# Two gate projections ahead of two x projections in each pair of a Mamba mixer kernel

## The chip, the cores and the metric

The kernel runs on one core of a Trainium2 chip. The metric is the device time of one execution in microseconds (us), lower is better. Five engines work side by side, each through its own list of instructions in order: PE is TensorE (matmuls), DVE is VectorE, ACT is ScalarE, POOL is GpSimd, and SP is SyncE, which issues the DMAs here. They wait for each other by counting semaphores.

## The reference

A residual stream x of 4 sequences of 256 tokens with 512 channels goes through a feed-forward layer, a Mamba2 mixer, and the same feed-forward layer again. Nearly all of the time is the mixer:

```python
proj = hidden_states @ in_proj_w.T
gate, xBC, dt = jnp.split(proj, [INTER, INTER + CONV_DIM], axis=-1)
...
xBC = jax.nn.silu(jnp.swapaxes(conv, 1, 2))
x, Bm, Cm = jnp.split(xBC, [INTER, INTER + NG * SS], axis=-1)
y = _ssd(x.reshape(Bsz, S, NH, HD), Bm.reshape(Bsz, S, NG, SS), Cm.reshape(Bsz, S, NG, SS), D, dt, dt_bias)
y = y.reshape(Bsz, S, INTER)
yg = y * jax.nn.silu(gate)
yg_g = yg.reshape(Bsz, S, NG, GROUP)
rstd = jax.lax.rsqrt(jnp.mean(jnp.square(yg_g), axis=-1, keepdims=True) + EPS)
out = (yg_g * rstd).reshape(Bsz, S, INTER) * norm_w
return out @ out_proj_w.T
```

INTER is 8192, in 8 groups of 1024 channels. `conv` is a causal convolution of 4 taps over the tokens, and `_ssd` the scan in chunks of 128 tokens, which inside a chunk is a product of a decay matrix, B and C, and x.

## The kernel before

The mixer goes through the 8 groups g. A group is 16 steps in 8 pairs j (`pair(g, j)`), and a tail (`tail`). A step is one tile of 128 channels of x and of the gate for half of the tokens (512 columns); the two steps of a pair, a = 2j and b = 2j + 1, are the two halves of one tile. Every engine has a `pair` and a `tail` of its own, which say in which order that engine does its work; nothing else orders it.

A projection is 12 matmuls of 128x512 (4 pieces of the contraction by three passes that split float32 into a high and a low part, `three_pass`, L166 to L168). There are two kinds in a pair:

- An x unit (`ip.project`, L923) writes bank 0 or 1. ACT starts the convolution (`evacuate`, L961), DVE adds three taps (`taps`, L976), ACT takes the tanh (L1337), DVE makes the silu (`silu_conv`, L1519) and turns the tile (L1529). It is sent out to HBM and comes back as `xd`, and POOL scales it (`scale_x`, L1253). The x units of a pair are those that the next pair mixes: steps 2j + 2 and 2j + 3. In the last pair of a group they are the next group's B and C units.
- A gate (`project_gate`, L1711) writes one of the two banks of `TG_BANK`. ACT takes the tanh (L1365) and DVE makes the silu (`silu_gate`, L1554). It waits for the weights (`wlo`), for the silu of the gate two steps before (`sg`), and, for the first two steps of a group, for `ms`, since the tail uses the same banks for sums (`turn_sums`, L1768), which DVE's `mean_square` reads (L1568) and whose last instruction (L1572) raises `ms`:

```python
pe.wait_ge(s["wlo"], 1 + WPG * g + w + 1)
if st < 2:
    pe.wait_ge(s["ms"], 1 + g)
if not (first(g) and st < 2):
    pe.wait_ge(s["sg"], 1 + STEPS * g + st - 1)
```

After these four PE does two output projections (`project_out`, 12 matmuls each; in group 0 there are none in pairs 0 to 3), for which POOL must have gated y (`gate_y`, L1232) and split the tile (`split_tile`, L1237), and then `mix_tokens` for a and b (L1737, L1741), which needs DVE's `make_mix` (L1540), ACT's decays (L1348, L1358) and `xd`. DVE then forms y (`skip_y`, L1548).

DVE's list for a pair is: `skip_y` of the two steps before, `make_mix` of a, `taps` of both x units, `make_mix` of b, then for each of the two a `silu_conv`, a `silu_gate` and a turn, then `split_wo` (L1558), and, in pairs 0 to 3, the sums `add_quads` and `add_group` (L995, L1002) of two tiles. In pair 0 both `make_mix` come ahead of the taps. In the tail it is: `skip_y` twice, constants, then

```python
taps(g + 1, 4)
taps(g + 1, 5)
mean_square(g)
```

and the silus of units 4 and 5. POOL's list for a pair is: two masks (L1224), `gate_y` twice, `split_tile` twice, `scale_x` twice, a mask (L1217), a weight remainder (L920), a mask, a weight remainder, and the squares' sums (L1245).

Of the kernel before, what the change touches and what calls it, by code (L numbers as in the profile page):

```python
# [163 lines left out]
def three_pass(nc, out, w_hi, w_lo, x_hi, x_lo, first, last):  # L164

    nc.tensor.matmul(out, w_hi, x_hi, start=first, stop=False)  # L166
    nc.tensor.matmul(out, w_hi, x_lo, start=False, stop=False)  # L167
    return nc.tensor.matmul(out, w_lo, x_hi, start=False, stop=last)  # L168
# [656 lines left out]
def first(g):  # L825

    return isinstance(g, int) and g == 0
# [205 lines left out]
def mixer_phase(nc, m, ip, norm_w, w_out, ncs_dram, x_dram, next_ln, sums, early):  # L1033

    with ExitStack() as ctx:
# [67 lines left out]
        def units_of(g, j):  # L1103

            if j < PAIRS - 1:
                return [(g, 2 * j + 6), (g, 2 * j + 7)]
            return [(g + 1, 0), (g + 1, 1)] if g + 1 < NG else []
# [12 lines left out]
        def has_tile(g, p):  # L1120
            return p >= XT or not first(g)
# [570 lines left out]
        def _(pe):  # L1692
# [18 lines left out]
            def project_gate(g, st):  # L1711
                w, hf = 3 + 2 * (st // 2), st % 2
# [5 lines that stand above are left out]
                at = slice(hf * HALF, (hf + 1) * HALF)  # L1718
                for k in range(KT):
                    last = three_pass(nc, TG_BANK[st % 2][:, :], w_hi[:, w % 3, k, :], w_lo[:, w % 3, k, :],  # L1720
                                      m.h_hi[:, k, at], m.h_lo[:, k, at], k == 0, k == KT - 1)
                last.then_inc(s["gate"], 1)

            def mix_tokens(g, st):

                i = st % 2
                x_scaled(pe, g, st)
                pe.wait_ge(s["mix"], 1 + STEPS * g + st + 1)
                if st == 0:
                    pe.wait_ge(s["cbt"], 1 + 2 * g + 1)  # L1730
                else:
                    pe.wait_ge(s["ysb"], 1 + STEPS * g + st - 1)
                for b in range(HB):
                    c0 = b * SEQ
                    for hd in range(2):
                        rows = slice(hd * HD, (hd + 1) * HD)
                        nc.tensor.matmul(Y_BANK[i][rows, c0:c0 + SEQ], xd[:, i, rows, 2 * b],  # L1737
                                         mix[:, i, hd, b, 0:SEQ], start=True, stop=False)
                    for hd in range(2):
                        rows = slice(hd * HD, (hd + 1) * HD)  # L1740
                        last = nc.tensor.matmul(Y_BANK[i][rows, c0 + CH:c0 + SEQ], xd[:, i, rows, 2 * b + 1],  # L1741
                                                mix[:, i, hd, b, SEQ:PAIR], start=False, stop=True)
                last.then_inc(s["y"], 1)

            def project_out(g, p):

                q = tile_of_step(p)[0]
                i, bank = p % 2, O_BANK[p % 2]
                pe.wait_ge(s["ylo"], 1 + STEPS * g + p + 1)
                pe.wait_ge(s["wolo"], 1 + XT * g + (QUAD if q == 0 else 0))  # L1750
                if p > XT + 1:
                    pe.wait_ge(s["gcopy"], 1 + TT * g + p - XT - 1)
                elif p >= 2:
                    pe.wait_ge(s["gsum"], 1 + TT * g + p - 1)
                elif g == NG:
                    pe.wait_ge(s["gcopy"], 1 + TT * g - 1 + p)
                else:
                    pe.wait_ge(s["cbt"], 1 + 2 * g + 2)
                for r in range(QUAD):
                    last = three_pass(nc, bank[:, :], yt_hi[:, i, r, :], yt_lo[:, i, r, :],  # L1760
                                      wo_hi[:, QUAD * q + r, :], wo_lo[:, QUAD * q + r, :], r == 0, r == QUAD - 1)
                last.then_inc(s["out"], 1)
# [13 lines left out]

            def pair(g, j):
                steps = (2 * j, 2 * j + 1)
                for u in units_of(g, j):
                    ip.project(pe, *u)  # L1780
                for st in steps:
                    project_gate(g, st)
                for p in steps:
                    if has_tile(g, p) and not (g == NG - 1 and p == STEPS - 1):
                        project_out(g, p)
                for st in steps:
                    mix_tokens(g, st)

            def tail(g, more):
# [9 lines left out]
                else:  # L1799
# [9 lines left out]
                    project_out(NG, 7)  # L1809

            groups_in_turn(pair, tail)


# [56 lines left out]
```

## Time and profile before

| | |
|---|---|
| median of 3 runs | 1524.92 us (1524.83 to 1527.4) |
| the profiled execution | 1522.31 us, its span 1520.5 us |
| PE busy | 1477.9 us |
| DVE busy | 1290.9 us |
| POOL busy | 1155.5 us |
| ACT busy | 1015.2 us |
| mean granted clock of PE | 0.991 of full |

Busy time is the time in which an engine has an instruction under way. Times in the rows are microseconds from the start of the span. A row of the timeline has the start, the time taken, the engine, the line in the kernel, the operation, what it writes and reads, and how many are merged; the square bracket at its end gives how long the engine had been idle and who released it.

### The profile page before, as it was taken

What the parts mean: (1) busy time and instruction counts of PE and PEld (TensorE: products, weight loads), DVE (VectorE), ACT (ScalarE), POOL (GpSimd) and SP (SyncE); (2) the same over time, 40 slices, a digit from 0 to 9 for tenths busy, and PEclk for the clock granted to TensorE, in tenths of its full rate; (3) what the DMA queues carried; (4) which work ended last, traced back from release to release, by engine and by line L of the source; (5) the groups of instructions that cost most, each with busy time, mean ns of one, the idle gap of its engine ahead of it and who ended that gap; (6) DMA issues with size and microseconds to landing.
All of it is one profiled execution on the core that took longest, in us unless ns stands there. A gap on an engine that the chain in (4) does not pass through costs nothing. (4 is left out here: it accounts for less than half of the span.)

```text
span 1520.5 us, 24373 instructions
## 1 busy us (share of the span) xinstructions
PE 1477.9 (97%) x7720; PEld 1212.3 (80%) x7720; DVE 1290.9 (85%) x1664; ACT 1015.2 (67%) x2154; POOL 1155.5 (76%) x917
## 2 busy tenths in 40 slices
PE   6979899999999999999999999999999999999988
PEld 4767788888888888888888888888888888888766
DVE  6689987998789987998789977998799987998675
ACT  4366777667766777667766677667766777667540
POOL 3017997699958997699959997699859997699830
PEclk9989999999999999999999999999999999999999
DMA  3026542444435442444434442544434442544201
GB/s 126 1 84 193 181 155 89 160 158 149 139 104 160 148 152 84 160 159 154 132 111 156 150 153 77 172 152 151 143 100 162 150 151 74 180 149 141 99 15 56
DMA packets 165680, 198.79 MB, mean 131 GB/s; under 512 B 21040, under 2 KB 86576, under 8 KB 165296
## 3 DMA queue, kind: packets, MB, share of 16 engines
q1 hardware_dynamic: 165552, 197.22, 39.5%
q8 instruction: 63, 1.03, 0.3%
q14 instruction: 65, 0.53, 0.1%
HBM read 160.98 MB, written 36.18 MB: 130 GB/s over the span
## 5 line engine op out<-in xcount | busy, mean ns | idle before, releaser
L166 PE MATMUL bank<-h_hi,mx_w_hi 128*128 128x512 f32 x1152 | 459.4, 399 | 4.4 <-DVE mx_acc L1519 2.8
L167 PE MATMUL bank<-h_lo,mx_w_hi 128*128 128x512 f32 x1152 | 450.3, 391 | 0.0
L168 PE MATMUL bank<-h_hi,mx_w_lo 128*128 128x512 f32 x1152 | 449.7, 390 | 0.0
L976 DVE SCALAR_TENSOR_TENSOR mx_acc<-bank,mx_cw,mx_acc 128x510 f32<-128x510 f32 (+2 forms) x480 | 353.9, 745 | 43.1 <-ACT mx_acc L961 29.9
L1540 DVE TENSOR_TENSOR mx_mix<-mx_mix,mx_cbt 128x1536 f32<-128x1536 f32 x128 | 266.0, 2083 | 37.0 <-ACT mx_mix L1358 37.0
L1348 ACT ACTIVATE mx_mix<-mx_csb,ncs 128x256 f32<-128x256 f32 x512 | 217.9, 498 | 111.1 <-PE bank L1741 109.1
L1232 POOL TENSOR_TENSOR mx_y<-mx_y,mx_sg 128x512 f32<-128x512 f32 x128 | 248.5, 1962 | 19.0 <-DVE mx_y L1548 19.0
L166 PEld LDWEIGHTS bank<-h_hi,mx_w_hi 128*128 128x128 f32 x1152 | 217.4, 189 | 56.0 <-POOL mx_w_lo L920 4.1
L168 PEld LDWEIGHTS bank<-h_hi,mx_w_lo 128*128 128x128 f32 x1152 | 217.1, 188 | 46.4
L167 PEld LDWEIGHTS bank<-h_lo,mx_w_hi 128*128 128x128 f32 x1152 | 217.6, 189 | 42.5
L920 POOL TENSOR_TENSOR mx_w_lo<-mx_w_raw,mx_w_hi 128x512 fp32r<-128x512 f32 x144 | 191.7, 1332 | 74.3 <-ACT mx_w_hi L915 73.8
L166 PE MATMUL bank<-mx_wo_hi,mx_yt_hi 128*128 128x512 f32 x512 | 201.0, 393 | 2.9 <-POOL mx_yt_lo L1237 2.9
L168 PE MATMUL bank<-mx_wo_hi,mx_yt_lo 128*128 128x512 f32 x512 | 200.2, 391 | 0.0
L167 PE MATMUL bank<-mx_wo_lo,mx_yt_hi 128*128 128x512 f32 x512 | 199.2, 389 | 0.0
L1217 POOL TENSOR_SCALAR_AFFINE_SELECT mx_csb<-mx_csb 128x512 f32<-128x512 f32 x128 | 119.6, 934 | 100.1 <-DMA mx_csb<-cs_rows 99.6
L1253 POOL TENSOR_TENSOR mx_xd<-mx_xd,mx_gdt 128x512 f32<-128x512 f32 x128 | 165.8, 1315 | 38.6 <-DMA mx_xd<-x_squares 38.6
L1237 POOL TENSOR_TENSOR mx_yt_lo<-mx_y,mx_yt_hi 128x512 fp32r<-128x512 f32 x128 | 167.2, 1325 | 30.4 <-ACT mx_yt_hi L1371 30.2
L1358 ACT ACTIVATE mx_mix<-mx_mix,ncs 128x128 f32<-128x128 f32 x512 | 162.7, 390 | 39.0 <-POOL mx_mix L1224 38.9
L1245 POOL TENSOR_TENSOR mx_ssum<-mx_ssum,mx_sq 128x512 f32<-128x512 f32 x112 | 175.0, 1582 | 0.1
L1737 PE MATMUL bank<-mx_mix,mx_xd 128*64 128x256 f32 x1024 | 163.4, 397 | 3.9 <-issue 3.1
L961 ACT ACTIVATE mx_acc<-bank,mx_cb,mx_cw 128x512 f32<-128x512 f32 x160 | 123.5, 773 | 53.4 <-PE bank L168 35.6
L1548 DVE SCALAR_TENSOR_TENSOR mx_y<-mx_acc,mx_dh,bank 128x512 f32<-128x512 f32 x128 | 92.4, 742 | 72.7 <-PE bank L1741 72.7
(172 smaller groups left out, 2236.8 us busy)
## 6 DMA issues: line engine op xcount, KB each, us to landing
mx_csb<-cs_rows SPq DMA_DIRECT2D x128, 512.0 KB, 4.1
mx_w_raw<-in_w_in SPq DMA_DIRECT2D x144, 256.0 KB, 3.7
x_squares<-mx_th SPq DMA_DIRECT2D x128, 256.0 KB, 2.0
mx_xd<-x_squares SPq DMA_DIRECT2D x512, 64.0 KB, 2.0
mx_wo_raw<-in_w_out SPq DMA_DIRECT2D x64, 256.0 KB, 4.2
res<-in_x SPq DMA_DIRECT2D x8, 256.0 KB, 4.4
out<-res SPq DMA_DIRECT2D x8, 256.0 KB, 2.0
f_base_raw<-in_base_wt SPq DMA_DIRECT2D x1, 1024.0 KB, 7.2
```

Of the source, the lines that this page charges most:

```text
L166: nc.tensor.matmul(out, w_hi, x_hi, start=first, stop=False)
L167: nc.tensor.matmul(out, w_hi, x_lo, start=False, stop=False)
L168: return nc.tensor.matmul(out, w_lo, x_hi, start=False, stop=last)
L920: self.nc.gpsimd.tensor_tensor(self.w_lo[:, w % 3, :, :], self.w_raw[:, w % 3, :, :], self.w_hi[:, w % 3, :, :].bitcast(F32), ALU.subtract ...
L976: self.nc.vector.scalar_tensor_tensor(dst, src[:, :, 0:SEQ - k], self.cw[:, c, TAPS - 1 - k:TAPS - k], dst, ALU.mult, ALU.add).then_inc(s[ ...
L1232: nc.gpsimd.tensor_tensor(y[:, st, :], y[:, st, :], sg[:, st % 2, :], ALU.mult).then_inc(s["yg"], 1)
L1237: nc.gpsimd.tensor_tensor(yt_lo[:, p % 2, :, :], y_tile(q, hf, t), yt_hi[:, p % 2, :, :].bitcast(F32), ALU.subtract).then_inc(s["ylo"], 1)
L1245: nc.gpsimd.tensor_tensor(ssum[:, i, :], ssum[:, i, :], sq[:, i, :], ALU.add).then_inc(s["ssum"], 1)
L1253: nc.gpsimd.tensor_tensor(a, a, gdt[:, hf, 2 * j:2 * j + 2, :].unsqueeze(2).to_broadcast([P, 2, HD, 2 * HB]), ALU.mult).then_inc(s["xd"], 1)
L1348: nc.scalar.activation(mix[:, i, hd, b, 0:SEQ], csb[:, i, hd, b * SEQ:(b + 1) * SEQ], ACT.Exp, bias=m.ncs[:, tile, head:head + 1], scale=-1.0)
L1540: nc.vector.tensor_tensor(a, a, both, ALU.mult).then_inc(s["mix"], 1)
L1737: nc.tensor.matmul(Y_BANK[i][rows, c0:c0 + SEQ], xd[:, i, rows, 2 * b], mix[:, i, hd, b, 0:SEQ], start=True, stop=False)
```

## The change

In PE's list for a pair, the two gate projections are written ahead of the two x units instead of behind them. No other engine's list changes, and no wait is added or removed.

```diff
             def pair(g, j):
                 steps = (2 * j, 2 * j + 1)
+                for st in steps:
+                    project_gate(g, st)
                 for u in units_of(g, j):
                     ip.project(pe, *u)
-                for st in steps:
-                    project_gate(g, st)
                 for p in steps:
                     if has_tile(g, p) and not (g == NG - 1 and p == STEPS - 1):
                         project_out(g, p)
```

PE's list where a tail ends and pair 0 of the next group begins (L1706 and L1707 are the last work of the tail; `mx_tap`, `mx_wlo`, `mx_sg` and `mx_ms` are the semaphores `tap`, `wlo`, `sg` and `ms`), before:

```order
L1706 MATMUL bank<-mx_acc 128x256 [waits mx_gcopy,mx_conv]
L1707 MATMUL bank<-mx_acc 128x128
L1706 MATMUL bank<-mx_acc 128x256
L1707 MATMUL bank<-mx_acc 128x128
L166 MATMUL bank<-h_hi,mx_w_hi 128x512 [waits mx_tap,mx_wlo]
L167 MATMUL bank<-h_lo,mx_w_hi 128x512
L168 MATMUL bank<-h_hi,mx_w_lo 128x512
```

And with the change:

```order
L1706 MATMUL bank<-mx_acc 128x256 [waits mx_gcopy,mx_conv]
L1707 MATMUL bank<-mx_acc 128x128
L1706 MATMUL bank<-mx_acc 128x256
L1707 MATMUL bank<-mx_acc 128x128
L166 MATMUL bank<-h_hi,mx_w_hi 128x512 [waits mx_sg,mx_ms,mx_wlo]
L167 MATMUL bank<-h_lo,mx_w_hi 128x512
L168 MATMUL bank<-h_hi,mx_w_lo 128x512
```

The first projection of the group was an x unit that waits for taps; now it is a gate that waits for `ms`. In the other pairs the last projection ahead of the output projections was a gate, before:

```order
L167 MATMUL bank<-h_lo,mx_w_hi 128x512
L168 MATMUL bank<-h_hi,mx_w_lo 128x512
L166 MATMUL bank<-h_hi,mx_w_hi 128x512 [waits mx_sg,mx_wlo]
L167 MATMUL bank<-h_lo,mx_w_hi 128x512
L168 MATMUL bank<-h_hi,mx_w_lo 128x512
```

And with the change it is the x unit of step b, which waits for the silu of the unit two before it (`mx_conv`):

```order
L167 MATMUL bank<-h_lo,mx_w_hi 128x512
L168 MATMUL bank<-h_hi,mx_w_lo 128x512
L166 MATMUL bank<-h_hi,mx_w_hi 128x512 [waits mx_conv,mx_wlo]
L167 MATMUL bank<-h_lo,mx_w_hi 128x512
L168 MATMUL bank<-h_hi,mx_w_lo 128x512
```

## Rows read from the trace of the kernel before

**Rows 1.** The page's busy time of each engine.

```profile
PE 1477.9 (97%) x7720; PEld 1212.3 (80%) x7720; DVE 1290.9 (85%) x1664; ACT 1015.2 (67%) x2154; POOL 1155.5 (76%) x917
```

**Rows 2.** Busy time by stretches; last three columns are clock, DMA share, GB/s.

```profile
173.40:1423.80 1250.40, 1250.36 (x6642) 1034.85 (x6640) 1098.74 (x1289) 878.77 (x1891) 1056.58 (x828) 1.00 0.43 140
```

**Rows 3.** Who waited for whom: total us, times, longest.

```profile
ACT mx_w_hi L915 <- PE bank L168: 88.6, 51, 2.2
```

**Rows 4.** Timeline of PE, pair 6 of group 3 and the next start.

```profile
724.08 0.50 PE L166 MATMUL bank<-h_hi,mx_w_hi 128*128 128x512 f32 x1
...
735.09 0.39 PE L166 MATMUL bank<-mx_wo_hi,mx_yt_hi 128*128 128x512 f32 x1
...
740.66 0.71 PE L1737 MATMUL bank<-mx_mix,mx_xd 128*64 128x256 f32 x4
...
743.52 0.50 PE L166 MATMUL bank<-h_hi,mx_w_hi 128*128 128x512 f32 x1
```

**Rows 5.** Timeline of ACT and DVE in the same pair.

```profile
729.85 0.78 ACT L961 ACTIVATE mx_acc<-bank,mx_cb,mx_cw 128x512 f32<-128x512 f32 x1 [0.35 <-PE bank L168]
...
730.66 2.31 DVE L976 SCALAR_TENSOR_TENSOR mx_acc<-bank,mx_cw,mx_acc 128x510 f32<-128x510 f32 x3 [0.41 <-ACT mx_acc L961]
732.89 2.26 DVE L1540 TENSOR_TENSOR mx_mix<-mx_mix,mx_cbt 128x1536 f32<-128x1536 f32 x1
...
735.67 0.67 DVE L1554 SCALAR_TENSOR_TENSOR mx_sg<-mx_sg,bank 128x512 f32<-128x512 f32 x1
...
739.36 1.12 DVE L1558 SCALAR_TENSOR_TENSOR mx_wo_lo<-mx_wo_raw,mx_nw,mx_wo_hi 128x512 fp32r<-128x512 f32 x1
```

**Rows 6.** Timeline of PE and DVE where group 4 begins.

```profile
777.45 0.48 PE L166 MATMUL bank<-h_hi,mx_w_hi 128*128 128x512 f32 x1
...
778.88 1.28 DVE L1568 TENSOR_REDUCE mx_rms<-bank 128x4 f32<-128x512 f32 x2
780.20 0.17 DVE L1572 TENSOR_SCALAR mx_rms<-mx_rms 128x8 f32<-128x8 f32 x1
```

**Rows 7.** The same place at the starts of groups 1 and 7.

```profile
267.16 0.48 PE L166 MATMUL bank<-h_hi,mx_w_hi 128*128 128x512 f32 x1
...
269.91 0.17 DVE L1572 TENSOR_SCALAR mx_rms<-mx_rms 128x8 f32<-128x8 f32 x1
...
1287.68 0.48 PE L166 MATMUL bank<-h_hi,mx_w_hi 128*128 128x512 f32 x1
...
1290.43 0.17 DVE L1572 TENSOR_SCALAR mx_rms<-mx_rms 128x8 f32<-128x8 f32 x1
```

**Rows 8.** Two idle times of PE in group 0, and a stretch's clock.

```profile
125.44 0.79 PE L166 MATMUL bank<-h_hi,mx_w_hi 128*128 128x512 f32 x1 [2.79 <-DVE mx_acc L1519]
...
129.84 0.40 PE L166 MATMUL bank<-h_hi,mx_w_hi 128*128 128x512 f32 x1
...
171.78 0.71 PE L1737 MATMUL bank<-mx_mix,mx_xd 128*64 128x256 f32 x4 [3.13 <-issue]
...
120.00:130.00 10.00, 7.21 (x43) 5.86 (x40) 9.41 (x14) 6.76 (x15) 7.39 (x8) 0.83 0.71 243
```

**Rows 9.** Timeline of group 0: DVE's first silu_gate, PE at pair 4.

```profile
123.19 0.68 DVE L1554 SCALAR_TENSOR_TENSOR mx_sg<-mx_sg,bank 128x512 f32<-128x512 f32 x1
...
173.41 0.80 PE L166 MATMUL bank<-h_hi,mx_w_hi 128*128 128x512 f32 x1
```

**Rows 10.** Timeline of DVE and POOL, pair 1 of group 4 into pair 2.

```profile
808.05 1.96 DVE L1540 TENSOR_TENSOR mx_mix<-mx_mix,mx_cbt 128x1536 f32<-128x1536 f32 x1
...
818.01 1.40 DVE L1548 SCALAR_TENSOR_TENSOR mx_y<-mx_acc,mx_dh,bank 128x512 f32<-128x512 f32 x2
...
818.84 4.08 POOL L1232 TENSOR_TENSOR mx_y<-mx_y,mx_sg 128x512 f32<-128x512 f32 x2 [1.62 <-DVE mx_y L1548]
822.86 2.58 POOL L1237 TENSOR_TENSOR mx_yt_lo<-mx_y,mx_yt_hi 128x512 fp32r<-128x512 f32 x2
```

**Rows 11.** Timeline of PE, the last pair of the last group.

```profile
1430.02 0.50 PE L166 MATMUL bank<-mx_wo_hi,mx_yt_hi 128*128 128x512 f32 x1 [0.48 <-POOL mx_yt_lo L1237]
```

## Prediction

> **What bounds the kernel now.** I read the page's busy times first: PE is busy 1477.9 us of 1520.5, far ahead of the others [rows 1]. Then I asked where its idle time lies. From pair 4 of group 0 to the last pair of group 7, 1250.4 us, PE is busy 1250.36 us at a granted clock of 1.00 [rows 2]. So for four fifths of the span PE's own work is the time: nothing can be gained there by order, and every wait that the change gives to PE is added in full. Next I read the timeline of one pair. It starts at 724.08, the four projections take 11.01 us (2.75 each), the output projections begin at 735.09, the mixing at 740.66, and the next pair starts at 743.52, 19.44 us after the first [rows 4]. Last I read, for each wait on PE, when it is satisfied today. Below, +n is the time since the start of a pair.
>
> **What the change does.** It removes and adds no instruction and no wait; PE, ACT, DVE, POOL and the DMA queue have the same work. Gates come 5.5 us earlier, x units 5.5 us later. ACT waits 88.6 us in all for PE ahead of a weight's rounding [rows 3], in good part because its list has that rounding behind the gates; those waits shorten, but with PE never idle in that stretch this is worth nothing, and ACT will wait ahead of its evacuations instead.
>
> *Term 1, the first gate of a group.* It waits for `ms`, raised by the last instruction of `mean_square`. At the start of group 4 the first projection runs at 777.45, while `ms` comes at 780.20 + 0.17 = 780.37, which is 2.92 us later [rows 6]. Today an x unit fills that time, whose taps are done. In group 1 the gap is 270.08 - 267.16 = 2.92 us and in group 7 1290.60 - 1287.68 = 2.92 us [rows 7]. The tail of each group is not reordered, and `mean_square` stands behind the taps of the last unit that the tail projects, so `ms` comes no earlier. PE's list is held at its head. The x units behind it are ready, but no row of this trace shows a matmul that passes one that waits. Seven group starts (1 to 7) by 2.92 give 20.4 us. Group 0 starts with `ms` free.
>
> The Trainium skill says of this ("TensorE: Matmul & The Clock Gate", the step-by-step part of Part 2) that matmuls stay in program order and only weight loads are pulled ahead. By that rule the term is the whole 20.4 us; if matmuls could pass each other it would be near nothing.
>
> *Term 2, the clock after such a gap.* PE was idle 2.79 us before 125.44, and the next projection took 129.84 - 125.44 = 4.40 us against 2.75, 1.65 us more; the stretch of 10 us around it has a mean granted clock of 0.83, so some 3.4 us at the lower level (1.2 GHz), 1.7 us of full-speed work lost [rows 8]. The gap of 3.13 us at 171.78 [rows 8] is followed by a first matmul of 0.80 us at 173.41 [rows 9], against 0.50 at 724.08 [rows 4]. So two of two gaps of this size in the mixer cost the clock. The new gap is 2.92 us. Bounds: nothing (each gap gets off) and 7 x 1.7 = 11.9; I take six of seven at 1.5, 9 us.
>
> The Trainium skill tells of such a loss paid at every pass of a loop ("TensorE: Matmul & The Clock Gate", HAM oscillation); its rule makes the loss hang on how long the gaps are. By it all seven would pay or hardly any; the two rows speak for paying.
>
> *Term 3, group 0, pairs 1 to 3.* Here there are no output projections to stand between the last x unit and the mixing. The mixing of b needs `make_mix` of b, which DVE has behind the taps of unit b. In pair 6 of group 3 the evacuation of unit b starts at 729.85, about 0.2 us after its projection, takes 0.78, the taps 2.3, `make_mix` 2.0 to 2.3 [rows 5]. With the unit's projection ending at +11.0, `make_mix` is done at about +16.3, the mixing of b (half of 743.52 - 740.66, 1.4 us [rows 4]) at +17.8. So these pairs take about 17.9 us. Pair 1 can begin when the first `silu_gate` is done, 123.19 + 0.68 = 123.9 [rows 9], instead of 125.44 [rows 8]; three pairs bring pair 4 to 177.6 instead of 173.41 [rows 9]: +4.2 us. PE is idle some 4 us in each of them, so the clock loss comes here too, about 1.2 each after what today's two gaps cost is gone: +8 us in all. Bounds -3 (the early start stays and the mixing is never late) and +12.
>
> *Term 4, output projections in pairs 2 to 4, groups 1 to 7.* DVE must now wait for the late x units and so does its later work later. From `make_mix` of b to the end of `skip_y` it takes 819.41 - 808.05 = 11.36 us where `add_quads` and `add_group` are in the list [rows 10]. `make_mix` of b starts at +14.3 (+11.0, 0.2, 0.78, 2.3 [rows 5]), so the first `skip_y` is done 24.9 us after the pair's start, +5.5 in the next. `gate_y` then takes 4.08 for two and the first split 1.3 [rows 10]: +10.9. PE wants it at +11.0 [rows 4]. The slack is 0.1 us. Today it is 3.1: the split is done at 822.86 + 1.3 = 824.2 [rows 10], +7.9 of a pair that starts at 777.45 + 2 x 19.44 = 816.3. POOL's list and its contention with DVE can shift it. There are 21 such pairs. Bounds: nothing, and 1 us each, 21; I take 0.15 each, 3 us, nearest the row.
>
> *Term 5, the last pair.* It has no x units, so its output projections want the split at about +5.6; today they start 0.48 us late, at 1430.02 [rows 11], which is +6.2. From `make_mix` of b to the end of `split_wo` DVE takes 740.48 - 732.89 = 7.6 us [rows 5]; +14.3 + 7.6 is +2.5 in the next pair, `skip_y` adds 0.7, `gate_y` and the first split 5.4: +8.6. That is 2.4 us later than today; I take 2.5. Bounds 0 and 5.
>
> *What stays covered.* In the other pairs, gate a needs `silu_gate` of the pair before: 3.45 us after the start of `make_mix` [rows 5], so at +17.8, ahead of 19.4. The mixing of b wants `make_mix` at +18.0 and gets it at about +16.5; the cover is the two output projections, 5.6 us, and without them it costs what term 3 says. The turned x of step a goes to its DMA soon after `silu_gate`, at about +19, and the mixing needs it at +16.6 of the next pair, 17 us on. The weights of a gate are split a pair ahead, those of x are now wanted later than before.
>
> The sum: 20.4 + 9 + 8 + 3 + 2.5 = 42.9 us. On the profiled execution, 1522.31 us, that is 1565.2. The median of the runs lies 2.6 us above the profiled one, so I forecast 1568 us.
>
> **Rivals.**
> - *The gap costs no clock.* 2.92 us may be too short in most groups, as it depends on what PE does around it. Then terms 2 and the clock's part of 3 fall away: 42.9 - 9 - 3.6 = 30.3, so 1555 us. For it: the gap of 2.92 is near the smaller of the two seen. Against: both of the two paid. Chance 0.22.
> - *POOL and DVE become the bound in pairs 1 to 4.* The slack of 0.1 us in term 4 is overrun by 1 us per pair, since POOL has two instructions of the same kind that take 1.3 us alone and 2 beside DVE [rows 10]. Then 28 pairs pay 1 us: 1568 - 3 + 28 = 1593 us. For it: POOL is busy 1056.58 us of 1250.4 [rows 2]. Against: that leaves 3 us per pair. Chance 0.12.
> - *Not slower: the gates fill group 0's holes and the group starts cost nothing.* If DVE reached `mean_square` 2.9 us earlier, relative to PE, than now, the first gate would find `ms` up. Then only group 0 changes: pair 1 starts 1.5 us earlier and its first projection keeps the clock, 1.65 us: 1522 us, 0.2% faster. It decides at 2.92 us of `ms` against the tail's end. Against it: three starts of groups, spread over the whole span, show the same 2.92 [rows 6, 7], and the tail's order is untouched. Chance 0.04, of which half would be within 0.2%.
>
> **How the numbers follow.** Forecast 0.62, rivals 0.22, 0.12, 0.04. The forecast's own spread is the bounds of term 2 (some 5 us down, 3 up), of term 3 (4 up) and of term 4 (10 up). The range 1549 to 1584 takes in the rival without clock loss and leaves out the other two, about 0.18. Measurements of this kernel tell 0.2%, 3 us, from no change. Slower 0.96, same 0.02, faster 0.02.
>
> **What would show it.** The waits of PE should have a new entry of about 2.9 us, seven times, the first matmul of a group released by DVE's L1572. The granted clock should show seven short falls between 260 and 1340 us. In group 0, PE should wait some 4 us ahead of L1737 in pairs 1 to 3, released by DVE's L1540. ACT's wait before L915 should shrink by some 50 us with PE no faster. Pair length in pairs 5 to 7 should stay at 19.44. I am wrong if `ms` is up when the tail ends, if pair lengths between group starts grow (POOL), or if the gaps leave the clock at 1.00.

## The result and the profile after

The changed kernel takes 1567.58 us (median of 4 runs, 1563.96 to 1569.85), the kernel before 1525.66 us on the same chip (4 runs, 1524.83 to 1527.40). The ratio is 1.0271, 95% interval [1.0248, 1.0294]: 2.7% slower. The forecast was 1568 us, range 1549 to 1584. The profiled execution of the changed kernel took 1568.67 us, with a span of 1566.9 us at a mean granted clock of 0.984; before, 1520.5 us at 0.991. So there are 46.4 us of span to account for.

The busy line of the changed kernel's page, which answers to [rows 1]:

```profile
PE 1491.8 (95%) x7720; PEld 1217.0 (78%) x7720; DVE 1277.4 (82%) x1664; ACT 1008.6 (64%) x2154; POOL 1136.2 (73%) x917
```

The counts are those of before. PE is busy 13.9 us longer with the same matmuls, which is what a lower clock looks like, and the rest of the 46.4 us is new idle time. The same instructions from pair 4 of group 0 to the last pair, which before took 1250.40 us [rows 2]:

```profile
184.20:1470.00 1285.80, 1260.88 (x6642) 1038.68 (x6640) 1081.42 (x1284) 871.72 (x1891) 1034.83 (x827) 0.99 0.43 136
```

This stretch is 35.4 us longer, 24.9 of them idle (1285.80 - 1260.88; before 0.04) and 10.5 more busy. The waits of PE in the whole changed kernel (total us, times, longest) name the idle time:

```profile
PE bank L166 <- issue: 19.4, 7, 2.8
PE bank L1737 <- issue: 10.2, 3, 3.4
PE bank L166 <- POOL mx_yt_lo L1237: 10.1, 9, 2.2
```

Seven waits ahead of a first gate, three ahead of a mixing in group 0, nine ahead of output projections. The kernel before has none of the first kind, one of the second (3.1 us) and three of the third (2.9 us). "issue" says only that the profile saw no releaser; the order of events shows it. This is the timeline of DVE and PE at the start of group 1, the place of [rows 7]:

```profile
277.14 2.31 DVE L976 SCALAR_TENSOR_TENSOR mx_acc<-bank,mx_cw,mx_acc 128x510 f32<-128x510 f32 x3 [0.24 <-ACT mx_acc L961]
279.37 1.28 DVE L1568 TENSOR_REDUCE mx_rms<-bank 128x4 f32<-128x512 f32 x2
280.69 0.17 DVE L1572 TENSOR_SCALAR mx_rms<-mx_rms 128x8 f32<-128x8 f32 x1
280.96 0.47 PE L166 MATMUL bank<-h_hi,mx_w_hi 128*128 128x512 f32 x1 [2.78 <-issue]
```

PE begins 0.10 us after `mean_square` ends (280.69 + 0.17 = 280.86), after an idle 2.78 us. The same picture stands at all seven starts.

PE's first matmul at pair 4 of group 0, at the starts of groups 2, 3, 4 and 7, and at the last output projections:

```profile
184.18 0.80 PE L166 MATMUL bank<-h_hi,mx_w_hi 128*128 128x512 f32 x1
...
455.39 0.47 PE L166 MATMUL bank<-h_hi,mx_w_hi 128*128 128x512 f32 x1 [2.77 <-issue]
...
629.79 0.47 PE L166 MATMUL bank<-h_hi,mx_w_hi 128*128 128x512 f32 x1 [2.78 <-issue]
...
805.79 0.77 PE L166 MATMUL bank<-h_hi,mx_w_hi 128*128 128x512 f32 x1 [2.77 <-issue]
...
1332.73 0.47 PE L166 MATMUL bank<-h_hi,mx_w_hi 128*128 128x512 f32 x1 [2.77 <-issue]
...
1478.01 0.50 PE L166 MATMUL bank<-mx_wo_hi,mx_yt_hi 128*128 128x512 f32 x1 [2.16 <-POOL mx_yt_lo L1237]
```

From these, with [rows 6, 7, 9, 11], the 46.4 us divide as follows. The shift against the kernel before is 184.18 - 173.41 = 10.77 at pair 4 of group 0, of which 0.55 was there before group 0 began. It is 280.96 - 267.16 = 13.80 at group 1, so 3.03 for one gap with its surroundings, 2.78 of it idle; at the six other starts it grows by 3.02. At group 7 it is 1332.73 - 1287.68 = 45.05, at the last outputs 47.99.

- Group 0: 10.77 - 0.55 = 10.2 us.
- Seven group starts: 7 x 3.02 = 21.1 us.
- The clock after them. From the first gate to the output projections, pair 0 takes 11.0 us (10.97 in group 1) where the clock stays, but in groups 3 to 6 it takes 12.60, 12.32, 12.61 and 12.56 us: 6.1 us more in all.
- Output projections of pairs 3 and 4 in groups 1 to 7: what is left of 47.99, so 47.99 - 0.55 - 10.2 - 21.1 - 6.1 - 1.7 = 8.3 us. Read pair by pair it is 8.6: these two pairs together are 1.3 to 1.4 us longer than before in six groups and 0.5 us in group 5; pairs 1 and 2 are not longer.
- The last pair: 2.16 - 0.48 = 1.7 us. In the two spans it does not show, since the part from there to the end of the span took 1520.5 - 1430.02 = 90.5 us before and 88.9 after.

That last line has nothing to do with the change. The same 368 matmuls of the end, before:

```profile
1430.00:1520.50 90.50, 78.23 (x368) 59.74 (x368) 53.65 (x124) 27.75 (x49) 28.79 (x22) 0.98 0.11 41
```

and after:

```profile
1478.00:1566.90 88.90, 76.54 (x368) 58.57 (x368) 53.66 (x124) 27.68 (x49) 28.76 (x22) 1.00 0.12 42
```

PE's busy time differs by 1.69 us at a granted clock of 0.98 against 1.00. The clock fell there in the profiled execution of before and not in that of after.

The clock after the gaps is seen in two windows of 14 us on the changed kernel, both around a group's start (group 2, then group 3; the clock is the third column from the end):

```profile
455.00:469.00 14.00, 13.61 (x60) 11.29 (x61) 10.68 (x14) 5.16 (x11) 4.11 (x4) 1.00 0.60 166
...
629.00:643.00 14.00, 13.21 (x51) 10.77 (x52) 9.53 (x11) 3.58 (x9) 3.73 (x3) 0.88 0.55 162
```

The idle time ahead is the same to 0.01 us, the work behind it too, and one keeps 2.4 GHz while the other falls to the 1.2 GHz level for some of the time and fits 51 matmuls instead of 60.

The wait at the output projections comes once in each of six groups (in pair 4 of groups 1, 2, 3 and 7, in pair 3 of groups 4 and 6, not in group 5). This is pair 4 of group 1, which starts at 358.89, with DVE and POOL ahead of it; the first three lines are the same instructions a pair earlier, in pair 3, which starts at 339.29:

```profile
339.05 3.00 POOL L1245 TENSOR_TENSOR mx_ssum<-mx_ssum,mx_sq 128x512 f32<-128x512 f32 x2
...
340.19 0.70 DVE L1558 SCALAR_TENSOR_TENSOR mx_wo_lo<-mx_wo_raw,mx_nw,mx_wo_hi 128x512 fp32r<-128x512 f32 x1
...
344.96 4.06 POOL L1232 TENSOR_TENSOR mx_y<-mx_y,mx_sg 128x512 f32<-128x512 f32 x2 [1.29 <-DVE mx_y L1548]
...
358.71 2.54 POOL L1245 TENSOR_TENSOR mx_ssum<-mx_ssum,mx_sq 128x512 f32<-128x512 f32 x2
...
360.01 1.79 DVE L1558 SCALAR_TENSOR_TENSOR mx_wo_lo<-mx_wo_raw,mx_nw,mx_wo_hi 128x512 fp32r<-128x512 f32 x1
...
364.80 1.40 DVE L1548 SCALAR_TENSOR_TENSOR mx_y<-mx_acc,mx_dh,bank 128x512 f32<-128x512 f32 x2
...
365.63 4.06 POOL L1232 TENSOR_TENSOR mx_y<-mx_y,mx_sg 128x512 f32<-128x512 f32 x2 [2.74 <-DVE mx_y L1548]
...
369.65 2.57 POOL L1237 TENSOR_TENSOR mx_yt_lo<-mx_y,mx_yt_hi 128x512 fp32r<-128x512 f32 x2
...
371.00 0.50 PE L166 MATMUL bank<-mx_wo_hi,mx_yt_hi 128*128 128x512 f32 x1 [0.94 <-POOL mx_yt_lo L1237]
```

POOL itself waited 2.74 us for DVE's `skip_y`: the engine that was late is DVE, not POOL, although PE's wait bears POOL's name. `gate_y` starts at +6.7 (365.63 - 358.89) and the output projections at +12.1 instead of +11.0.

DVE's lateness has two parts. It creeps: `gate_y` starts at +5.1, +5.3 and +5.7 in pairs 1 to 3. Then it jumps to +6.7, and the jump of 1.07 us is that of one instruction: `split_wo` (L1558) takes 1.79 us in place of 0.70. POOL's two sums of squares (L1245) run beside it both times; what differs is which began first. At 340.19 the first sum had 0.15 us to go, and it was the second sum that took 1.74 us. At 360.01 the second sum had begun 0.04 us before, took its 1.29 us, and `split_wo` ended 0.54 us after it. In all six groups in which PE waits, the `split_wo` before that wait took 1.76 to 1.84 us; in pairs 1 to 4 of group 5 none took more than 1.16 us, and PE had no wait. (Two more of 1.8 us, in group 0 and in pair 5 of group 4, came where DVE was 2 us less late and cost nothing.) No run moved `split_wo` by itself.

### The profile page after: what moved, and what is told of

Same layout as the page of the kernel before. It is cut to its first block and busy times, and to the rows that moved or that the text cites. A ratio compares the mean times of both kernels' runs of the same rounds, so it can differ in the third digit from the quotient of the medians.

```text
span 1566.9 us, 24373 instructions
## 1 busy us (share of the span) xinstructions
PE 1491.8 (95%) x7720; PEld 1217.0 (78%) x7720; DVE 1277.4 (82%) x1664; ACT 1008.6 (64%) x2154; POOL 1136.2 (73%) x917
## 5 line engine op out<-in xcount | busy, mean ns | idle before, releaser
L976 DVE SCALAR_TENSOR_TENSOR mx_acc<-bank,mx_cw,mx_acc 128x510 f32<-128x510 f32 (+2 forms) x480 | 357.9, 746 | 158.6 <-ACT mx_acc L961 147.1
L166 PE MATMUL bank<-h_hi,mx_w_hi 128*128 128x512 f32 x1152 | 462.5, 401 | 21.1 <-issue 19.4
L920 POOL TENSOR_TENSOR mx_w_lo<-mx_w_raw,mx_w_hi 128x512 fp32r<-128x512 f32 x144 | 240.8, 1673 | 104.4 <-ACT mx_w_hi L915 104.2
L1540 DVE TENSOR_TENSOR mx_mix<-mx_mix,mx_cbt 128x1536 f32<-128x1536 f32 x128 | 262.2, 2053 | 46.1 <-ACT mx_mix L1358 46.1
L961 ACT ACTIVATE mx_acc<-bank,mx_cb,mx_cw 128x512 f32<-128x512 f32 x160 | 124.4, 778 | 270.1 <-PE bank L168 250.6
L166 PEld LDWEIGHTS bank<-h_hi,mx_w_hi 128*128 128x128 f32 x1152 | 219.2, 190 | 74.5 <-issue 23.7
L166 PE MATMUL bank<-mx_wo_hi,mx_yt_hi 128*128 128x512 f32 x512 | 202.4, 395 | 10.1 <-POOL mx_yt_lo L1237 10.1
L1737 PE MATMUL bank<-mx_mix,mx_xd 128*64 128x256 f32 x1024 | 166.1, 403 | 12.0 <-issue 10.2
L1217 POOL TENSOR_SCALAR_AFFINE_SELECT mx_csb<-mx_csb 128x512 f32<-128x512 f32 x128 | 95.6, 747 | 106.9 <-DMA mx_csb<-cs_rows 105.8
L1245 POOL TENSOR_TENSOR mx_ssum<-mx_ssum,mx_sq 128x512 f32<-128x512 f32 x112 | 166.5, 1508 | 0.0
L1253 POOL TENSOR_TENSOR mx_xd<-mx_xd,mx_gdt 128x512 f32<-128x512 f32 x128 | 132.1, 1051 | 39.9 <-DMA mx_xd<-x_squares 39.8
L1529 DVE STREAM_TRANSPOSE mx_th<-mx_acc 128x512 f32<-128x512 f32 x128 | 147.4, 1152 | 0.6
```

Source lines behind the costliest of these rows:

```text
L920: self.nc.gpsimd.tensor_tensor(self.w_lo[:, w % 3, :, :], self.w_raw[:, w % 3, :, :], self.w_hi[:, w % 3, :, :].bitcast(F32), ALU.subtract ...
L976: self.nc.vector.scalar_tensor_tensor(dst, src[:, :, 0:SEQ - k], self.cw[:, c, TAPS - 1 - k:TAPS - k], dst, ALU.mult, ALU.add).then_inc(s[ ...
L1245: nc.gpsimd.tensor_tensor(ssum[:, i, :], ssum[:, i, :], sq[:, i, :], ALU.add).then_inc(s["ssum"], 1)
L1540: nc.vector.tensor_tensor(a, a, both, ALU.mult).then_inc(s["mix"], 1)
```

## Experiments

Each kernel starts from the changed one, or from the one before where it says so, and was timed with the kernel before on the same chip. "x first" is the order of before. The edits of `pair` are written as conditions under which a pair projects its x units first; in all other pairs the gates come first.

**1. Group starts put back.** The changed kernel, but

```diff
+                if j == 0 and g > 0:      # x first here
+                    for u in units: ip.project(pe, *u)
```

> The changed kernel, but in pair 0 of groups 1 to 7 the x units come ahead of the gates again. Theory (the first gates wait for ms, 7 x 2.8 to 3.0 us, and four to five of these gaps cost the clock 1.5 us each): 27 us less than the changed kernel, about 1540 us, no wait of PE of 2.8 us left at a group start, clock at 1.00 there. Rival (late x units hold DVE and POOL back everywhere, and the wait at the group start only shows where that is paid): the time stays within 10 us of 1567, the waits turn up elsewhere.

1539.83 us, before 1522.35, ratio 1.0113 [1.0098, 1.0129]. The wait `L166 <- issue` is gone from PE's list; those of group 0 and of the outputs stay:

```profile
PE bank L1737 <- issue: 10.2, 3, 3.4
PE bank L166 <- POOL mx_yt_lo L1237: 8.2, 8, 2.2
```

Seven of 64 pairs hold more than half of the loss.

**2. The opposite: gates first only in pair 0 of groups 1 to 7.**

```diff
+                if not (j == 0 and g > 0):      # x first here
```

> The kernel before, with the gates ahead of the x units only in pair 0 of groups 1 to 7. Theory: seven waits of 2.8 us and some lost clock, 1525.7 + 21 + 6 = 1553 us, group 0 and the output projections of pair 4 as before. Rival (losses of late x units in all pairs): 1530 us or less.

1555.14 us, before 1522.35, ratio 1.0215 [1.0200, 1.0230]: +32.8 us from seven pairs. PE's new wait is `L166 <- issue`, 19.4 us, 7 times, as in the changed kernel. The windows at three of the starts:

```profile
268.00:284.00 16.00, 13.78 (x54) 11.23 (x55) 11.16 (x14) 4.80 (x11) 4.53 (x4) 0.89 0.47 150
792.00:808.00 16.00, 14.06 (x62) 11.66 (x63) 12.68 (x16) 6.68 (x13) 4.22 (x4) 1.00 0.47 133
1315.00:1331.00 16.00, 14.87 (x53) 12.03 (x54) 9.89 (x13) 4.32 (x11) 3.97 (x4) 0.79 0.47 146
```

Here six of seven starts show the lower clock, all but the one at 792. Where the clock falls, the pair's projections take 12.35 to 12.60 us, at the last start 13.83, against 11.0: 10.3 us more in all. Experiments 1 and 2 together lose 17.5 + 32.8 = 50.3 us, 8 more than the changed kernel's 41.9. In the profiled spans the surplus is 3.8 us (17.4 + 32.8 against 46.4), about what six falls (10.3 us) cost more than four (6.1). The rest lies within the intervals: that of the changed kernel's loss alone goes from 37.8 to 44.8 us.

**3. Is it `ms`?** In the changed kernel's DVE list, the tail of a group:

```diff
+                    mean_square(g)
                     taps(g + 1, 5)
-                    mean_square(g)
```

> The changed kernel, with DVE's mean_square ahead of the taps of the tail's last unit, so that ms comes some 2.3 us earlier against the same PE list. Theory: PE's wait at the group start shrinks from 2.8 to about 0.5 us, no gap is left that lowers the clock: 7 x 2.3 + 6 = 22 us less, about 1545 us. Rival (the first gate waits for its weights or for the gate of two steps before and not for ms): no change from 1567.

1542.71 us, before 1522.35, ratio 1.0136 [1.0121, 1.0151]. PE and DVE at the start of group 1:

```profile
271.86 1.27 DVE L1568 TENSOR_REDUCE mx_rms<-bank 128x4 f32<-128x512 f32 x2
...
273.17 0.17 DVE L1572 TENSOR_SCALAR mx_rms<-mx_rms 128x8 f32<-128x8 f32 x1
...
273.44 0.47 PE L166 MATMUL bank<-h_hi,mx_w_hi 128*128 128x512 f32 x1 [0.22 <-issue]
```

The gates are still first, `ms` comes 2.3 us earlier (it no longer stands behind taps of 2.31 us), and the wait falls from 2.78 to 0.22 us. So the wait was for `mean_square`, and it was late only by its place in DVE's list.

**4. One x unit as cover.** In pair 0 of groups 1 to 7 one x unit goes ahead of the gates (x, gate, gate, x):

```diff
+                if j == 0 and g > 0:
+                    ip.project(pe, *units.pop(0))
```

> The changed kernel, with one x unit ahead of the two gates in pair 0 of groups 1 to 7 (x, gate, gate, x). Theory: the x unit fills 2.75 of the 2.9 us until ms; PE waits under 0.3 us and the clock stays: 1540 us, as with both units ahead. Rival (the gap is more than the wait for ms): more than 1545.

1542.68 us, before 1523.43, ratio 1.0126 [1.0113, 1.0140]. No wait at the starts; the window at the first:

```profile
273.00:287.00 14.00, 14.00 (x65) 11.40 (x64) 13.04 (x17) 6.42 (x14) 4.75 (x5) 1.00 0.30 90
```

2.75 us of work that is ready [rows 4] is nearly as long as the lateness of 2.92 us, and leaves no gap that is seen. Its interval overlaps those of experiments 1 and 3.

**5. The wait without the clock's loss, all pairs.** Ahead of the first gate of groups 1 to 7, PE gets twelve matmuls that nobody uses, as soon as the ones ahead of them are done:

```diff
+                if j == 0 and g > 0:
+                    pe.wait_ge(s["wlo"], 1 + WPG * g + 4)
+                    pe.wait_ge(s["cbt"], 1 + 2 * g + 1)
+                    for k in range(12):
+                        nc.tensor.matmul(Y_BANK[0][:, :], w_hi[:, 0, k % KT, :], m.h_hi[:, k % KT, 0:HALF], start=True, stop=True)
```

> The changed kernel, with 12 extra matmuls of 128x512 (2.7 us) in front of the first gate of groups 1 to 7; their result lies in a bank that is overwritten later and is used by nothing. The gap until ms stays as long and is filled with work that gives nothing. Theory (part of the loss is the clock that falls after the gap): 6 to 12 us less than the changed kernel, 1556 to 1562 us, no half clock at a group start. Rival (the clock costs nothing by itself, only the wait counts): the same time as the changed kernel or a little more.

1558.11 us, before 1522.87, ratio 1.0240 [1.0226, 1.0254]. The changed kernel's ratio is 1.0271 [1.0248, 1.0294]: useless work in the gap makes it about 5 us faster (0.0031 x 1523), though the two intervals overlap. The traces say the same with a caution: the seven gaps have no lower clock any more, but group 0, where nothing differs, took 72.6 us from its first projection to pair 4 against 76.1 in the changed kernel's trace. So this pair of kernels alone would not settle it.

**6. The same in the kernel of experiment 2.**

> The same 84 matmuls in the kernel that has the gates first only in pair 0 of groups 1 to 7 (1555.1 us, 33 us above the kernel before). Theory: 7 x 2.9 us of waiting stay, the clock's 12 us go: 1523 + 20 to 21 = 1544 us. Rival (nothing from the clock): 1555.

1542.91 us, before 1522.87, ratio 1.0135 [1.0121, 1.0149], against 1.0215 [1.0200, 1.0230] with empty gaps. The window around the first start:

```profile
265.00:285.00 20.00, 20.00 (x94) 16.41 (x93) 16.21 (x20) 9.82 (x19) 6.77 (x6) 1.00 0.35 107
```

PE has no idle time there and the clock stays at 1.00. With the gap filled the seven starts cost 1542.91 - 1522.87 = 20.0 us, 2.9 each: the pure lateness. With it empty they cost 32.8 us. The 12.2 to 12.8 us between them (0.0080 x 1523; 32.8 - 20.0) is the clock, and this is the cleanest measurement of it here. In the two traces the starts alone differ by 10.5 us (31.4 and 20.8 us above the kernel before), and group 0 by 0.5.

**7. Gates first only in pairs 4 to 7, all groups.**

```diff
+                if j < XT // 2:      # x first here
```

> The kernel before, with the gates ahead of the x units only in pairs 4 to 7 of each group, the pairs in which DVE has no add_quads and add_group. Theory (DVE's list fits there, its lateness is caught up within the next pair; only the last pair of the last group pays, some 2 us): 1524 to 1526 us beside 1523 for the kernel before, pairs of 19.45 us. Rival (late x units cost a little in every pair): half of the 8 us of the output projections' waits, 1528 or more.

1524.90 us (12 runs), before 1523.14, ratio 1.0008 [0.9997, 1.0019]: no change that can be told. In half of the pairs the new order is free. The one wait that answers to it is at the last pair's outputs, as in the changed kernel:

```profile
PE bank L166 <- POOL mx_yt_lo L1237: 4.0, 3, 2.2
```

**8. Gates first only in pairs 1 to 3 of groups 1 to 7.**

```diff
+                if g == 0 or j not in (1, 2, 3):      # x first here
```

> The kernel before, with the gates first only in pairs 1 to 3 of groups 1 to 7, where DVE's list has the sums. Theory (its lateness adds up over these pairs and comes out as a wait of PE for POOL's split in pair 3 or 4): seven waits of about 0.6 to 0.95 us and the lengthening around them, 7 to 8 us more than before, 1530 us. Rival (the wait belongs to pair 4's own order): 1525 us or less.

1530.60 us, before 1523.14, ratio 1.0047 [1.0033, 1.0061]: +7.5 us. PE's wait for the split, once or so a group:

```profile
PE bank L166 <- POOL mx_yt_lo L1237: 7.7, 10, 1.7
```

With experiments 1 and 7 this leaves group 0: 17.5 - 7.5 - 1.8 = 8.2 us. Each of the three has an interval of some 2 us to either side, so it is a rough figure.

**9. Group 0 put back.**

```diff
+                if g == 0 and j < XT // 2:      # x first here
```

> The changed kernel, with the x units first in pairs 0 to 3 of group 0, the pairs without output projections. Theory: the three waits of 3.4 us ahead of the mixing and their half clock go, 10 us less, about 1557 us; groups 1 to 7 as in the changed kernel. Rival (group 0 only started later and its length is set by POOL and the DMAs): under 3 us.

1563.33 us (1555.18 to 1565.67), before 1522.35, ratio 1.0273 [1.0252, 1.0293]. The expectation of 1557 was missed: by the ratio nothing was won. Yet in its trace group 0 is back in time; pair 4 starts here, against 184.18 in the changed kernel:

```profile
174.28 0.53 PE L166 MATMUL bank<-h_hi,mx_w_hi 128*128 128x512 f32 x1
```

That is 9.9 us less. Its profiled execution had a span of 1553.1 us at a clock of 0.990. Another execution of the same kernel had 1563.5 us at 0.984. A mean of 0.006 less over 1560 us is 9.4 us of full-speed work lost, and the spans differ by 10.4. In the trace only two of the seven starts lose the clock. So the 10 us that group 0 gave back stand in the trace, and in most timed runs the clock's loss was larger than in the profiled one. That more starts fell in those runs is argued from the mean clock alone; no trace of them shows which. The 9.9 us are also more than group 0 is worth as a rule, since the changed kernel's profiled group 0 was a slow one (see term 3 below).

**10. Can group 0 be mended from the other side?** The theory: `make_mix` of b could stand ahead of the taps of b, so that a late x unit doesn't make it late. ACT's decays of b move ahead of its evacuations, and DVE's list becomes

```diff
                 make_mix(g, a)
+                make_mix(g, b)      # in every pair, ahead of the taps of b
...
-                if j > 0:
-                    make_mix(g, b)
```

> The changed kernel, with the decays of step b ahead of the evacuations in ACT's list and make_mix of b ahead of the taps in DVE's. Theory (in group 0 the mixing of b waits for a make_mix that stands behind late taps; in pair 4 the output projection waits for a DVE list that ends 2 us too late): both go, 10 + 8 us less, about 1549 us, with the waits at the group starts left. Rival (POOL is the cause in pair 4, by its weight remainders beside DVE's make_mix): only group 0's 10 us go, 1557.

1604.27 us (1596.95 to 1604.81), before 1523.43, ratio 1.0520 [1.0499, 1.0542]: the worst kernel here. The waits ahead of the mixing in group 0 are gone (pair 4 starts at 174.65), but PE has new ones, in every group, beside the seven at the group starts (first line):

```profile
PE bank L166 <- issue: 19.4, 7, 2.8
PE bank L166 <- POOL mx_yt_lo L1237: 18.0, 26, 3.0
PE bank L166 <- POOL mx_w_lo L920: 14.8, 7, 2.1
...
PE bank L166 <- DVE mx_sg L1552: 5.6, 4, 1.9
PE bank L166 <- DVE mx_acc L1517: 5.4, 7, 1.3
```

**11. The same with x first at the group starts** (the condition of experiment 1).

> As the run before, and x units first in pair 0 of groups 1 to 7. Theory: all four losses gone, and the gates ahead of the x units may fill group 0's two old gaps of PE: 1519 to 1525 us. Rival (the lists of ACT and DVE are worse in the middle groups): above 1530.

1573.58 us, before 1523.43, ratio 1.0330 [1.0314, 1.0347]. A miss as well; but 30.7 us below experiment 10, so the group starts cost here about what they cost in experiment 2.

**12. The lists of experiment 10 in the kernel before.**

> The kernel before (x units first everywhere) with the same lists of ACT and DVE as the two runs before. Theory: evacuations come 3 us later with x first, the taps follow, but PE has the slack of two gates and two output projections in groups 1 to 7: 1522 to 1530 us. If it is as fast as the run before, what that one wins comes from the lists and not from the gates' place.

1565.96 us, before 1523.43, ratio 1.0275 [1.0257, 1.0293]. The lists alone cost 42.5 us, with PE's order as it was. Among all waits of this kernel the largest is ACT's:

```profile
ACT bank L1337 <- DVE mx_acc L976: 244.4, 125, 5.6
DVE mx_mix L1538 <- ACT mx_mix L1358: 118.3, 80, 2.4
```

DVE runs `make_mix` of b, waits 118.3 us in all for ACT's part of it, and reaches its taps later, for which ACT then waits 244.4 us; the weights and the gates behind them come late, and PE waits 20.8 us for POOL's weight remainders and 12.6 us for its split. That this chain is the cause is read from the waits and was not tried alone. The theory that `make_mix` of b had room ahead of the taps has fallen.

None of these kernels is faster than the kernel before; the nearest is experiment 7, equal to it within 0.2%.

## Why the prediction was right

**Term 1, the first gate of a group: right.** Put at 7 x 2.92 = 20.4 us. Measured 21.1 in the trace (7 x 3.02, 19.4 idle) and 20.0 with the gap filled (experiment 6). Experiments 1, 3 and 4 take it away in three ways. The matmuls of the x units, ready behind the waiting gate, did not pass it: 2.78 us idle with ready work behind is the row that was missing before.

**Term 2, the clock: right in kind, not constant in size.** Put at 9 us as six falls of 1.5. The profiled execution had four, worth 6.1 (1.3 to 1.6 each), near the 5 us that experiment 5 won back; in experiment 2, with six falls in its trace, the seven starts lose 10.3 us in that trace and 12 to 13 by the medians, about at my upper bound of 11.9. The rival "the gap costs no clock" (1555 us) is refuted by experiment 6; experiment 5 agrees. That "two of two" gaps of this size cost the clock was too small a sample: of 28 such gaps in four traces 14 do.

**Term 3, group 0: near.** Put at 8 us, 10.2 in the trace, 8.2 (roughly) from the medians. PE waits 3.40 us in each of the pairs 1 to 3 ahead of L1737 behind `make_mix` of b, and the first of them reads:

```profile
140.99 1.13 PE L1737 MATMUL bank<-mx_mix,mx_xd 128*64 128x256 f32 x4 [3.40 <-issue]
```

The three pairs from 124.90 to 184.18 take 19.8 us each instead of the 17.9 put. I had given `make_mix` of b as done at +16.3, which is met: the one in pair 1 starts at 139.14 and takes 1.75, so it ends at 140.89, +16.0. What I undersized for this execution is the clock behind each wait. The first four matmuls of the mixing take 1.13 us against 0.71 in [rows 4]. Without its 3.40 us idle a pair takes 16.4 us for four projections and a mixing that take 11.01 + 2.86 = 13.9 at full speed [rows 4]: 2.5 us more per pair, where I put 1.2. Pair 1 also began at 124.90 and not at 123.9, because DVE's first `silu_gate` was done 0.9 us later than before. The window over group 0 up to pair 4 has a mean granted clock of 0.89:

```profile
107.70:184.20 76.50, 63.85 (x325) 50.26 (x324) 62.95 (x73) 50.00 (x113) 47.15 (x40) 0.89 0.49 153
```

Other executions bring the term back to what I put. From the first projection of group 0 to pair 4 the order of the changed kernel takes 76.1 us here, but 72.5 to 73.8 in the traces of experiments 1, 3, 4 and 5, which have the same order there. The order of before takes 65.1 to 67.2 us over six traces (the kernel before and experiments 2, 6, 7, 8 and 9). The means differ by 7.5 us.

**Term 4, the output projections: right place, mis-sized.** Put at 21 x 0.15 = 3 us, with a slack of 0.1 us; the trace has 8.3 to 8.6, experiment 8 7.5. It is no equal toll of every pair. The lateness of DVE creeps up by 0.6 us from pair 1 to 3, which uses up the slack, and then PE's wait comes out once in six of the groups, 0.8 to 1.0 us, with smaller stretches beside it. What sets its size is a duration that I took as fixed: from [rows 5] `split_wo` takes 1.12 us, but it took 0.70 when POOL's sum was about to end and 1.76 to 1.84 when one had just begun (above). The rival that POOL or DVE becomes the bound in these pairs had this mechanism, at 28 us; it is there at less than a third of that. In the pairs 4 to 7 the order is free (experiment 7), as stated under what stays covered.

**Term 5, the last pair: small and right.** Put at 2.5, measured 1.7. It doesn't show in the span's end, because the profiled execution of the kernel before lost 1.7 us to the clock in that part.

**The rival that ends not slower** wanted `ms` 2.9 us earlier relative to PE. It is not up earlier, and experiment 3 shows that even then the rest of the change costs 1.4%.

The terms sum to 42.9 us; the medians differ by 41.9 and the profiled spans by 46.4. Part of the closeness is luck: term 4 was put 5 us too small and term 2 for the profiled run 3 too large. I also added 2.6 us because the median before lay above the profiled execution; after the change it lies 1.1 us below. And one kernel's executions lie up to 10 us apart.

**The signs.** The seven waits came, without a releaser's name. The falls of the clock were four, not seven. PE's waits ahead of L1737 were 3.4 us, not 4. ACT's 88.6 us ahead of the weights' rounding are gone and its wait ahead of the evacuations grew from 35.6 to 250.6 us, worth nothing as said. Pairs 5 to 7 kept their 19.44 us. One sign of being wrong, longer pairs between the group starts, came in part: pairs 3 and 4.

**Left open.** Which starts lose the clock in a given execution, and why those; whether all of the 8 us by which experiments 1 and 2 exceed the changed kernel are clock and noise; and whether moving `split_wo` away from POOL's sums would take the wait of pairs 3 and 4 away.

## What to carry to other kernels

Where one engine is busy without a hole, ask of each wait that is moved ahead when it is satisfied today, counting from the same mark as the work; a wait that only the first turn of a loop carries (here `ms`) is easily missed, and held more than half of the loss. The cheap cures are to leave one ready piece of work ahead of it or to move the producer ahead of what it needn't follow; both gave back nearly 1.5%. A slack of 0.1 us on a chain over three engines is none: let the lateness add up over the pairs, and price an instruction that shares its time with another engine's by its longest row (`split_wo`: 0.70 to 1.84 us), for a shift of half a microsecond can decide which of the two waits.

## What the runs showed of the hardware that I had not expected

- The same idle time has two outcomes. With 2.77 or 2.78 us idle ahead and the same matmuls behind, TensorE kept 2.4 GHz at the starts of groups 1, 2 and 7 of the changed kernel and fell to 1.2 GHz for a while at those of groups 3 to 6. Over the four kernels with this gap it fell at two (experiments 9 and 10), four (the changed kernel) and six (experiment 2) of seven starts. One kernel's executions spread by 10 us with it (spans of 1553.1 us at 0.990 and 1563.5 at 0.984).
- Twelve useless matmuls in each gap made the kernel of experiment 2 12 us faster (1.0215 to 1.0135). They don't shorten the wait; they keep the clock. The Trainium skill gives idle gaps as the cause of a clock that falls at every pass of a loop ("TensorE: Matmul & The Clock Gate", HAM oscillation). The trace agrees only in part: seven gaps of 2.77 or 2.78 us, and four falls.
- The same DVE instruction (`split_wo`, 128x512) took 0.70 us in one pair of the changed kernel and 1.79 us in the next, beside the same two sums of POOL. In these rows the instruction that began second is the one that took longer: POOL's second sum took 1.74 us where `split_wo` had begun 0.12 us before it, and 1.29 us where it had itself begun 0.04 us before `split_wo`. The same shows in a longer case: POOL's remainder of a weight took 2.80 us where DVE's `make_mix` had begun before it (353.54, 2.22 us), and 1.29 us three microseconds later:

```profile
354.10 2.80 POOL L920 TENSOR_TENSOR mx_w_lo<-mx_w_raw,mx_w_hi 128x512 fp32r<-128x512 f32 x1
...
357.47 1.29 POOL L920 TENSOR_TENSOR mx_w_lo<-mx_w_raw,mx_w_hi 128x512 fp32r<-128x512 f32 x1
```
